# Down weights loaded per expert during the last attention batch, and the last batch's routing scatter moved ahead of tile 1's results

## The reference, cut to what matters

```python
x = x + attn_a(layernorm(x), ...)
x = x + ffn(layernorm(x), router_w, Wg, Wu, Wd)
x = x + attn_b(layernorm(x), ...)
x = x + ffn(layernorm(x), router_w, Wg, Wu, Wd)

# ffn: H = 256, I = 688, E = 8 experts, TOPK = 2
logits = xf @ router_w.T
top_vals, top_idx = lax.top_k(logits, 2)
top_w = softmax(top_vals)
for e in range(E):
    h = silu(xf @ Wg[e].T) * (xf @ Wu[e].T)
    y = h @ Wd[e].T
    out = out + combine[:, e:e+1] * y
```

## Time and profile before

| | |
|---|---|
| median of 3 runs | 930.68 us (930.08 to 937.3) |
| the profiled execution | 930.45 us, span 928.7 us |
| PE busy | 793.1 us, 85% of the span |
| DVE, ACT, POOL busy | 365.0, 290.4, 225.2 us |
| PE share of the chain that ended last | 74% |
| DMA share of that chain | 8% |

### The profile page before, as it was taken

The page is one execution under the profiler, slowest core; times in us unless marked ns, Lnnn a source line. Parts: engine busy times, 40 slices in busy tenths (PEclk is TensorE's granted clock), DMA queues, the critical chain, the costliest instruction groups (busy, mean ns, idle before and its releaser), DMA issues.

```text
span 928.7 us, 14805 instructions
## 1 busy us (share of the span) xinstructions
PE 793.1 (85%) x5020; PEld 603.6 (65%) x5021; DVE 365.0 (39%) x902; ACT 290.4 (31%) x527; POOL 225.2 (24%) x262
## 2 busy tenths in 40 slices
PE   1989799999975989999983459989897989999990
PEld 1767587777753767777762337767675767777760
DVE  8444164543532412222135575666533422212212
ACT  1102104114322234334323205445463244434321
POOL 8341013343040241221222500003213242112212
PEclk9999899999987999999995879999998999999995
DMA  6963914124638026101103451112122020011004
GB/s 195 409 140 111 321 42 104 45 53 118 283 99 207 23 70 215 54 24 33 68 18 96 120 155 34 33 33 68 61 97 63 18 75 27 30 34 34 29 17 142
DMA packets 47029, 88.19 MB, mean 95 GB/s; under 512 B 8700, under 2 KB 36732, under 8 KB 44860
## 3 DMA queue, kind: packets, MB, share of 16 engines
q1 hardware_dynamic: 34000, 48.92, 18.4%
q0 software_dynamic: 9008, 36.60, 11.6%
q10 hardware_dynamic: 3968, 1.97, 0.8%
HBM read 52.33 MB, written 35.13 MB: 94 GB/s over the span
## 4 chain that ended last, share of the span: by engine, by line
PE 74%; DMA 8%; DVE 8%; issue 6%; POOL 2%; ACT 1%; SPq 0%; ACTq 0%; POOLq 0%; DVEq 0%
PE bank L1377 22%; PE bank L1404 13%; PE bank L880 9%; PE bank L1390 3%; PE bank L459 3%; PE bank L504 3%; DMA R<-in_wd 3%; PE bank L515 2%; PE bank L449 2%; PE bank L533 2%; PE bank L502 2%; DVE XN L596 2%; DMA PTR<-rows_out 2%; DVE stat L324 2%; PE bank L550 1%
## 5 line engine op out<-in xcount | busy, mean ns | idle before, releaser
L1377 PE MATMUL bank<-wgu,R 128*128 x736 | 224.6, 458 | 0.0
L1377 PEld LDWEIGHTS bank<-wgu,R 128*128 128x128 f32 x736 | 137.7, 193 | 64.7 <-issue 2.4
L1404 PE MATMUL bank<-R 112*128 (+1 forms) x552 | 129.5, 385 | 12.1 <-DMA R<-in_wd 10.8
L1404 PEld LDWEIGHTS bank<-R 112*128 112x128 f32 (+1 forms) x552 | 106.1, 193 | 34.0 <-issue 12.8
L1442 DVE TENSOR_TENSOR R<-R,bank 128x344 f32<-128x344 f32 x92 | 47.2, 513 | 180.8 <-PE bank L1377 172.8
L647 ACT ACTIVATE PTR<-bank 128x512 f32<-128x512 f32 x144 | 83.5, 597 | 97.7 <-PE bank L504 82.5
L1353 POOL DMA_INDIRECT rows_out<-R,XN x46 | 45.5, 989 | 191.0 <-ACT R L1434 179.8
L1449 DVE COPY R<-bank 112x512 f32<-112x512 f32 x46 | 31.7, 690 | 104.2 <-PE bank L1390 104.2
L1434 ACT ACTIVATE R<-bank 128x256 f32<-128x256 f32 x46 | 17.6, 383 | 160.3 <-PE bank L1404 160.3
L596 DVE TENSOR_REDUCE XN<-bank 128x2 f32<-128x512 f32 x96 | 63.1, 685 | 10.9 <-PE bank L459 10.9
L1420 ACT ACTIVATE R<-bank 128x344 f32<-128x344 f32 x92 | 41.8, 457 | 75.4 <-PE bank L1377 75.2
(11 more groups left out here) (169 smaller groups left out, 1280.9 us busy)
## 6 DMA issues: line engine op xcount, KB each, us to landing
wgu<-in_wgu SPq DMA_DIRECT2D x10, 1376.0 KB, 11.4
slots_in<-PTR POOLq DMA_DIRECT2D x1, 9088.0 KB, 26.1
row_of_slot<-in_unused POOLq DMA_DIRECT2D x2, 4544.0 KB, 17.7
R<-slots_in SPq DMA_DIRECT2D x46, 128.0 KB, 2.0
wgu<-R SPq DMA_DIRECT2D x32, 128.0 KB, 2.4
R<-R SPq DMA_DIRECT2D x32, 128.0 KB, 2.4
PTR<-rows_out SPq DMA_DIRECT2D x16, 256.0 KB, 3.2
R<-in_wd POOLq DMA_DIRECT2D x1, 3584.0 KB, 18.5
```

Source lines behind the costliest of these rows:

```text
L1377: last = nc.tensor.matmul(BK[2 * half + gu][:, 0:IH], xsT[:, p, kk, :], wgu[:, bass.ds(e * (KD * GU) + (kk * GU + gu * I + half * IH), IH) ...
L1404: last = nc.tensor.matmul(down_bank(i)[:, 0:D], hT[0:CH[c], p, c, :], wd[0:CH[c], bass.ds(e * (6 * D) + c * D, D)], start=c == 0, stop=c == 5)
```

## The change

The two large DMAs of the down weights on POOL's queue become sixteen on SP's: `load_down(e)` loads one expert in two DMAs (0.46 MB in 112 rows of 4 KB, 0.25 MB in 120 rows of 2 KB), as soon as its columns are free. Experts 6 and 7 lie in the staging buffers and are loaded behind gate/up 3; experts 0 and 3 after two of batch 3's four groups, expert 1 after three, and experts 2, 4 and 5 after the last, behind the loads of the first two tiles. PE's wait for all of them keeps its place. The value loads of `expert_of`, five in a row ahead of the first tile in both layers, are spread, each ahead of the tile that needs it. In both layers POOL scatters batch 3's rows between the results of tiles 0 and 1 instead of between those of 1 and 2.

```diff
--- before.py
+++ after.py
@@ -1217,7 +1217,6 @@
             out_t_tensor(a, b, heads(a)[0] - 1)
             nc.tensor.wait_ge(FF[l]["eid"], 1)
             nc.tensor.wait_ge(s_wgu, 16 * (E if l == 1 else E + 2))
-            e = [expert_of(i) for i in range(FULL_T)]
 
             def hidden_and_next(i, n, p):
                 tile_hidden(l, i, n, p, range(4))
@@ -1226,26 +1225,30 @@
 
             tile_transpose(l, 0, 0, 0)
             tile_transpose(l, 1, 0, 1)
+            e = [expert_of(0)]
             tile_up(l, 0, 0, 0, e[0], [0])
             all_t_tensor(a, b)
             tile_up(l, 0, 0, 0, e[0], [1])
             project_tensor(a, b)
+            e.append(expert_of(1))
             hidden_and_next(0, 0, 0)
             tile_up(l, 1, 0, 1, e[1])
             norm_tensor(l, b)
-            nc.tensor.wait_ge(s_wd, 32)
+            nc.tensor.wait_ge(s_wd, 2 * E * 16)
             tile_down(l, 0, 0, 0, e[0])
             logits_tensor(l, b)
+            e.append(expert_of(2))
             hidden_and_next(1, 0, 1)
             tile_up(l, 2, 1, 0, e[2], [0])
             rank_tensor(l, b)
             tile_up(l, 2, 1, 0, e[2], [1])
             tile_down(l, 1, 0, 1, e[1])
+            e.append(expert_of(3))
             hidden_and_next(2, 1, 0)
             tile_up(l, 3, 1, 1, e[3])
             tile_down(l, 2, 1, 0, e[2])
-            tile_hidden(l, 3, 1, 1, range(4))
-            tile_hidden(l, 3, 1, 1, range(4, 6))
+            e.append(expert_of(4))
+            tile_hidden(l, 3, 1, 1)
             tile_up(l, 4, 2, 0, e[4])
             tile_down(l, 3, 1, 1, e[3])
             nc.tensor.wait_ge(FF[l]["eid"], 2)
@@ -1504,6 +1507,10 @@
             nc.sync.wait_ge(s["scatter1"], 64)
             load_tile(l, 0, 0, 0, first[0])
             load_tile(l, 1, 0, 1, first[1])
+            if l == 1:
+                nc.sync.wait_ge(AT[0]["shifted"], B * GA * 3)
+                for e in (2, 4, 5):
+                    load_down(e)
             tile_sync(l, 0, 0, 0)
             tile_sync(l, 1, 0, 1)
             tile_sync(l, 2, 1, 0)
@@ -1523,8 +1530,8 @@
             load_rows(l, 0, 0)
             load_rows(l, 1, 1)
             tile_gpsimd(l, 0, 0, 0)
+            scatter_gpsimd(l, B - 1)
             tile_gpsimd(l, 1, 0, 1)
-            scatter_gpsimd(l, B - 1)
             tile_gpsimd(l, 2, 1, 0)
             nc.gpsimd.wait_ge(s["eid"], 2)
             nc.gpsimd.wait_ge(s["rows"], 16 * (TOPK * NT + 1))
@@ -1581,13 +1588,10 @@
             nc.sync.dma_start(wgu[:, e * KD * GU:(e + 1) * KD * GU].rearrange("p (k n) -> p k n", k=KD),
                               dr["wgu"][e].rearrange("(k p) n -> p k n", p=P)).then_inc(s_wgu, 16)
 
-        def load_down_gpsimd():
-            nc.gpsimd.wait_ge(AT[0]["shifted"], B * 3 * GA)
-            nc.gpsimd.wait_ge(PA["placed_k"], B * PLACED_K)
-            nc.gpsimd.wait_ge(AT[0]["placed"], B * PLACED_A)
-            wdv = R1[:, :].rearrange("p (e m) -> p e m", e=E)
-            nc.gpsimd.dma_start(wdv[0:CH[0], :, 0:4 * D], dr["wd4"].rearrange("e p m -> p e m")).then_inc(s_wd, 16)
-            nc.gpsimd.dma_start(wdv[0:CH[5], :, 4 * D:6 * D], dr["wd2"].rearrange("e p m -> p e m")).then_inc(s_wd, 16)
+        def load_down(e):
+            at = R1[:, e * 6 * D:(e + 1) * 6 * D]
+            nc.sync.dma_start(at[0:CH[0], 0:4 * D], dr["wd4"][e]).then_inc(s_wd, 16)
+            nc.sync.dma_start(at[0:CH[5], 4 * D:6 * D], dr["wd2"][e]).then_inc(s_wd, 16)
 
         def route_consts_sync(l):
             s = FF[l]
@@ -1628,10 +1632,17 @@
             sp.wait_ge(PA["placed_k"], B * PLACED_K)
             sp.wait_ge(AT[0]["placed"], B * PLACED_A)
             load_gate_up(3)
+            load_down(6)
+            load_down(7)
             sp.wait_ge(AT[0]["pv"], (B - 1) * GA)
             sp.wait_ge(FF[1]["scatter0"], 64)
             sp.wait_ge(FF[1]["scatter1"], 64)
             load_gate_up(4)
+            sp.wait_ge(AT[0]["shifted"], ((B - 1) * GA + 2) * 3)
+            load_down(0)
+            load_down(3)
+            sp.wait_ge(AT[0]["shifted"], ((B - 1) * GA + 3) * 3)
+            load_down(1)
             experts_sync(1)
             sp.wait_ge(PA["evac_v"], B * len(BY_V))
             sp.dma_start(rope[:, :, :], dr["rope_b"]).then_inc(s_const, 16)
@@ -1673,7 +1684,6 @@
                 if b > 1:
                     scatter_gpsimd(1, b - 2)
             scatter_gpsimd(1, B - 2)
-            load_down_gpsimd()
             experts_gpsimd(1)
             combine_gpsimd(1)
             pool.wait_ge(AT[0]["pv"], B * GA)
```

## The result

The changed kernel takes **916.94 us** (median of 4 runs, 914.97 to 919.7) against 931.98 for the kernel before in the same session (930.08 to 937.3): ratio 0.9839, 95% interval 0.9808 to 0.9871. The forecast was 915 in a range of 911 to 920, worked out as 15.6 us less than before; the medians say 15.0. A second time, beside the experiments, it took 916.53 us, ratio 0.9834 (0.9814 to 0.9854). The profiled execution took 916.41 us with a span of 914.2, against 930.45 and 928.7.

The account below looks back on a forecast made before the run. PE's mixture-layer matmuls led the chain, with PE idle in layer 1 for value loads and down weights. Terms 10.8 + 2.5 + 2.3 + 0 = 15.6 us off 930.45 gave 914.85, or 915 us, range 911 to 920.

Parts of the forecast that it names:

- The wait (-10.8): Layer 1, first `tile_down`: PE's wait for the down weights goes to 0, 10.8 us less.
- its clock (-2.5): Layer 1, first `tile_down`: no longer at half clock, 2.76 us instead of 5.28, 2.5 us less.
- The rate of the pieces: Down weights on SP's queue: between 215 and 423 GB/s, taken nearer the gate/up loads' 423; no wait at either end.
- The value loads (-2.3): Layer 1, ahead of tile 0: with value loads spread, gate/up matmuls start at 272.95 instead of 275.24, 2.3 us less.
- Layer 3 (0): Layer 3, ahead of tile 0: the value loads hide behind the tile's rows, so spreading them gains 0.
- The scatter (0): POOL, both layers: tile 1's result goes out later, ACT has its buffer with 6.5 us to spare; 0.
- The clock did not stay up by itself (0.18): Rival, after the last attention step: PE's clock doesn't fall or is back earlier, 913.2 or 911.5 us; chance 0.18.
- The fixed cost in turn (0.09): Rival, down-weight loads: each piece pays its fixed cost in turn, 5.1 us an expert, 920 us; chance 0.09.
- SP's queue did clog: Rival, SP's queue: pieces under 107 GB/s lose the gain, at 80 GB/s the time is 948 us; chance 0.04.

Follow-up runs that it names:

- The loads alone: Changed kernel with the five value loads in a row and the scatter where they were before; 917.70 us, ratio 0.9841 to the kernel before.
- matmuls of no use: Changed kernel with extra matmuls into a free bank, in PE's idle time around the transposes of tiles 0 and 1; 916.52 us, ratio 0.9837 to before.
- the scatter alone: Kernel before with only batch 3's scatter moved ahead of tile 1's result, in both layers; 931.64 us, ratio 0.9985.
- the sixteen pieces late on SP's queue: Kernel before with down weights in sixteen pieces on SP's queue, all issued behind the rows of tiles 0 and 1; 934.80 us, ratio 1.0008.
- the change again: The whole changed kernel measured a second time, on the same chip as its parts; 916.53 us, ratio 0.9834 to the kernel before.
- the value loads alone: Kernel before with only the value loads spread as in the change, weights on POOL's queue and scatter as before; 932.27 us, ratio 0.9989.

## Why the prediction was right, step by step

**The wait (-10.8) and its clock (-2.5).** Right. The loads alone shortened layer 1's stage by 14.2 us against these 13.3. The rest comes ahead of `tile_down`, where the two profiles start their gate/up matmuls 0.3 us apart and run them in 3.62 and 3.91 us. That difference in length is no effect of the loads: it lies within what this length varies by from profile to profile, as the part on the value loads shows. SP's queue with the late experts' first and last issue, and the last by its source view:

```profile
268.90 0.43 SPq L1593 DMA_DIRECT2D R<-in_wd  x1
...
271.45 0.47 SPq L1594 DMA_DIRECT2D R<-in_wd  x1
```

```profile
L1594 SPq DMA_DIRECT2D R<-in_wd x1: 472/472/472, 271.5 to 271.5; - x1
...
DMA to landing us min/median/max: 8.6/8.6/8.6
```

It landed 8.6 us later, at 280.1, inside the 275 to 281 named, 7.5 us ahead of its use.

**The rate of the pieces.** My reason was wrong though the term was not. I took something nearer the gate/up loads, "since queue and direction are theirs". Windows of 2 us of the changed kernel, while gate/up, expert 0 and 3, and the late experts move:

```profile
240.00:242.00 2.00, 2.00 (x13) 1.64 (x12) 1.43 (x3) 0.00 (x0) 0.00 (x0) 1.00 1.02 424
...
256.00:258.00 2.00, 2.00 (x13) 1.45 (x12) 0.86 (x5) 0.60 (x1) 0.00 (x0) 1.00 0.97 285
...
272.00:274.00 2.00, 1.72 (x4) 1.09 (x4) 0.00 (x0) 1.67 (x2) 0.00 (x0) 0.50 1.08 302
```

424, then 285 and 302: nearer the lower bound of 215. The queue has no part in it (26.8 and 27.3 us for the same two loads), the partitions do. The early issue left so much room that the step came out at 0 from either end, which is why the bounds were worth working out and the choice between them was not.

**The value loads (-2.3).** Right in the start, mis-sized in what it gave. The start of the gate/up matmuls moved as forecast, by 2.03 us in one profile and 2.32 in the other (5.45 against 3.42 and 3.13). But the term also carried their length over as 3.91 us, without a reason. They took 4.88 us, and 4.03 in the second profile, and of 2.3 us, 0.45 and 1.37 were left against the loads alone (21.61 less 21.16 and 20.24). No run shows that the earlier start costs this. The length varied about as much where the start had not moved. In the eight profiles with the five value loads in a row it lies between 3.56 and 4.79 us, in the three with them spread and no matmuls of no use it is 3.77, 4.03 and 4.88. The two ends of the eight, from the scatter alone and from the sixteen pieces late on SP's queue:

```profile
274.04 3.56 PE L1377 MATMUL bank<-wgu,R 128*128 x8
```

```profile
278.33 4.79 PE L1377 MATMUL bank<-wgu,R 128*128 x8
```

What differs is when the clock fell in the same gap. Windows of 0.5 us of the loads alone and of the change again, and the change again's first gate/up matmuls:

```profile
273.50:274.00 0.50, 0.38 (x2) 0.14 (x2) 0.00 (x0) 0.08 (x1) 0.00 (x0) 0.79 1.04 250
```

```profile
273.00:273.50 0.50, 0.50 (x4) 0.30 (x3) 0.00 (x0) 0.50 (x1) 0.00 (x0) 0.94 1.05 283
```

```profile
272.47 4.03 PE L1380 MATMUL bank<-wgu,R 128*128 x8 [0.67 <-ACT R L1415]
```

Before, it fell at 271.3, 1.1 us after PE's last matmul had ended (the prediction's 1.5 counts from that matmul's start). In the loads alone it stayed up for 3.6 us of idle time and fell at 273.8; in the change again it fell at 273.4, a microsecond after the gate/up matmuls had begun; in the change's first profile at 270.3. What sets that moment stays open. So the length differs from one execution to the next, with a spread of 1.3 us in layer 1, and a profile of before shows only one of its values; the sum had no term for it. In the medians nothing of the value loads can be told from zero. That the time still came within 2 us of 915 is in part luck: the loads' stage came out 0.9 us above their 13.3, and this covers part of what is missing here.

**Layer 3 (0).** Right in the main: 0.3 and 0.7 us longer. Tile 0's rows release the transposes, after 3.65 and 3.10 us (3.16 before), and with one value load between them the matmuls start 2.01 us behind the transposes and not 1.70.

**The scatter (0).** Right. POOL in the changed kernel, from its row loads to tile 1's result, and ACT's copy of tile 3's result:

```profile
279.27 0.59 POOL L1348 DMA_DIRECT2D XN<-row_of_slot  x1 [7.88 <-issue]
...
296.26 1.02 POOL L1322 DMA_INDIRECT slots_in<-XN,stat  x1 [0.55 <-DVE stat L1159]
...
305.30 0.97 POOL L1325 DMA_INDIRECT row_of_slot<-wb,stat  x1 [0.30 <-issue]
306.57 0.97 POOL L1356 DMA_INDIRECT rows_out<-R,XN  x1 [0.30 <-issue]
```

```profile
316.41 0.38 ACT L1437 ACTIVATE R<-bank 128x256 f32<-128x256 f32 x1 [1.77 <-PE bank L1407]
```

Tile 1's result goes out at 306.57, right behind the scatter, has landed by 310.2, and ACT wants its buffer at 316.41: 6.2 us to spare, where 6.5 were forecast. One thing I missed: the row loads of tiles 0 and 1, at 275.02 before, now start at 279.27, 8.9 us after the last issue of batch 2's row numbers instead of 3.8. POOL waits there for the landing of these, which now lies beside the late experts; that this makes it slow is argued, not tested. The rows are used at 291.6, so it costs nothing.

**The rivals.** The clock did not stay up by itself (0.18), in either layer. The fixed cost in turn (0.09) fell with the sixteen late pieces at 250 GB/s, 2.8 us an expert where it had 5.1. SP's queue did clog in one sense that my rival had missed: at 250 GB/s it isn't the weights that come late but the small loads behind them, by 10 to 12 us if all are issued at once. The change escapes this because only three of the eight experts are still to be moved when the third tile's rows are issued.

## What to carry to other kernels

A large load that must wait for its memory need not wait for all of it: cut by what frees first, most of it moved here while PE was busy, and the other queue did nothing without that, the smaller size 2 us. Rows in all 128 partitions did more, 7.4 us with the loads still late. Before such loads go on the queue that also feeds the tiles, count what stands behind them. And don't carry over the length of the first matmuls behind an idle stretch from one profile: it differs from one execution to the next, here between 3.5 and 4.9 us, and belongs in the range.

## What the runs showed of the hardware

- A load into 112 and 120 partitions moved at about 250 GB/s, into 128 at 412 (same 4 and 2 KB rows, same queue, same stretch), and at 427 with 6 KB rows. The DMA engines' busy share was 1.02 to 1.04 in the windows shown of all three, so a share of 1 does not tell that they move all they can.
- The same two loads took 26.8 us to land from SP's queue and 27.3 from POOL's; cut into sixteen, PE's wait on POOL's queue fell from 10.8 to 8.9 us.
- After the attention's last transposes the granted clock fell to half in each of the eleven profiles without matmuls of no use, in both layers, also where PE was idle for no more than 0.58 us ahead of tile 0 (the value loads alone), and in none of the three in which such matmuls filled the gap. With them the first eight gate/up matmuls took 2.48 us instead of 3.48 to 4.88.
- The moment of the fall varied: in layer 1 it came 1.1 us after PE went idle (before), 3.6 us after (the loads alone), or only when PE had been at work again for a microsecond (the change again).
